# Last tower layer of a Fourier network: two of the square convolutions moved to its very beginning, one into each mix step, and unread TensorE products on both sides of the join

## The reference

```python
for i in range(L):                                   # L = 4
    x1 = _fourier_layer(v, W1, W2)                   # rfft2, 12 x 12 modes mixed, irfft2
    x2 = jnp.einsum('bcxy,cd->bdxy', v, w_w[i]) + w_b[i][None, :, None, None]
    v = x1 + x2
    mean = jnp.mean(v, axis=(0, 2, 3), keepdims=True)
    var = jnp.var(v, axis=(0, 2, 3), keepdims=True)
    v = (v - mean) * jax.lax.rsqrt(var + BN_EPS)
    v = v * bn_g[i][None, :, None, None] + bn_b[i][None, :, None, None]
    if i < L - 1:
        v = jax.nn.relu(v)
out = jnp.einsum('bcxy,cu->bxyu', v, q_w) + q_b
```

## Time and profile before

| | us |
|---|---|
| median of 3 runs | 854.49 (853.65 to 860.16) |
| profiled execution, its time | 850.2 |
| profiled execution, its span | 848.4 |
| TensorE busy | 665.2 (78%) |
| VectorE busy | 561.2 (66%) |
| ScalarE busy | 361.2 (43%) |
| L696 (convolutions, 512 instructions), busy | 45.6 |

### The profile page before, as it was taken

How to read it: one execution, slowest core, us unless ns; L and a number is a source line. 1 busy time by engine, 2 the same in 40 slices (tenths; PEclk the granted TensorE clock), 3 DMA queues, 4 the chain that set the end, 5 groups by cost and what they waited for, 6 DMA issues and landing times. The chain is left out here.

```text
span 848.4 us, 22240 instructions
## 1 busy us (share of the span) xinstructions
PE 665.2 (78%) x10155; PEld 443.9 (52%) x10155; DVE 561.2 (66%) x858; ACT 361.2 (43%) x485; POOL 49.6 (6%) x88
## 2 busy tenths in 40 slices
PE   3889927776899276678992999777967979797997
PEld 2867613336676132376761334234365858685854
DVE  7859878973688799736887797224047675547453
ACT  0025569100255591002555775331034646364753
POOL 3100000002000000110000000200010202010200
PEclk9989968996899699958996899755987989677999
DMA  8400000023000000320000000400040000000001
GB/s 303 92 2 3 3 0 2 1 87 141 2 2 2 1 1 2 129 98 2 3 2 1 2 2 2 150 20 3 14 179 1 3 1 1 1 1 1 1 1 27
DMA packets 12270, 27.28 MB, mean 32 GB/s; under 512 B 3472, under 2 KB 4368, under 8 KB 12176
## 3 DMA queue, kind: packets, MB, share of 16 engines
q1 hardware_dynamic: 11888, 25.12, 8.8%
q10 hardware_dynamic: 288, 0.73, 0.2%
HBM read 24.80 MB, written 1.05 MB: 30 GB/s over the span
## 5 line engine op out<-in xcount | busy, mean ns | idle before, releaser
L438 ACT ACTIVATE V<-ps,wts 128x1024 f32<-128x1024 f32 x96 | 101.8, 1111 | 252.8 <-PE ps L784 252.8
L612 DVE BATCH_NORM_STATS2 stats<-V 128x6 f32<-128x512 f32 x192 | 117.9, 676 | 15.8 <-ACT V L438 15.6
L488 DVE STREAM_TRANSPOSE A<-V 128x2048 f32<-128x2048 f32 x48 | 107.2, 2273 | 6.7 <-ACT V L389 6.7
L684 PE MATMUL ps<-A,tab 128*128 128x384 f32 x192 | 75.4, 532 | 30.6 <-DVE A L495 30.6
L389 ACT ACTIVATE V<-V,small 128x2048 f32<-128x2048 f32 x48 | 96.6, 2082 | 5.0 <-DVE small L640 5.0
L672 PE MATMUL ps<-A,tab 32*32 32x512 f32 x1536 | 66.6, 654 | 33.8 <-DVE A L488 33.8
L606 DVE STREAM_TRANSPOSE A<-ps 128x2048 f32<-128x2048 f32 x24 | 55.5, 2315 | 36.2 <-PE ps L769 36.1
L684 PEld LDWEIGHTS ps<-A,tab 128*128 128x128 f32 x192 | 36.0, 201 | 80.7 <-DVE A L495 57.4
L784 PEld LDWEIGHTS ps<-tab,A 64*128 64x128 f32 x1024 | 62.5, 195 | 28.0 <-issue 28.0
L495 DVE STREAM_TRANSPOSE A<-ps 128x1024 f32<-128x1024 f32 x48 | 56.7, 1220 | 20.1 <-PE ps L672 20.1
L784 PE MATMUL ps<-tab,A 64*128 64x128 f32 x1024 | 68.8, 286 | 0.0
(11 more groups left out here) (229 smaller groups left out, 919.6 us busy)
## 6 DMA issues: line engine op xcount, KB each, us to landing
A<-in_modes SPq DMA_DIRECT2D x32, 384.0 KB, 6.5
r_ky<-in_modes SPq DMA_DIRECT2D x16, 384.0 KB, 6.4
wl<-in_layers SPq DMA_DIRECT2D x3, 452.0 KB, 5.7
wm<-in_mixture SPq DMA_DIRECT2D x1, 874.5 KB, 8.0
tab<-in_table SPq DMA_DIRECT2D x1, 656.5 KB, 4.9
A<-in_turned SPq DMA_DIRECT2D x1, 512.0 KB, 3.9
V<-in_pixels SPq DMA_DIRECT2D x4, 128.0 KB
tower_out<-A SPq DMA_DIRECT2D x2, 256.0 KB, 2.0
```

The costliest lines, as they stand in the source:

```text
L438: nc.scalar.activation(Vm[:, 2 * h:2 * h + 2, r, 512 * q:512 * (q + 1)], bank(half_of_u(q, r) + 2 * h, 2).rearrange("p (m n) -> p m n", m= ...
L488: nc.vector.transpose(T[n % 3].rearrange("p (k n) -> p k n", k=16), Vk[:, :, P * n:P * (n + 1)]).then_inc(s_T, 1)
L612: last = nc.vector.bn_stats(stats[:, 16 * q + 4 * r + m, :], Vm[:, m, r, 512 * q:512 * (q + 1)])
L684: last = nc.tensor.matmul(bank(4 + (2 * (u % 2) if l < L - 1 else 0) + pair)[:, 0:MODES * CH], fwd_x[layout][ri], y[:, :, MODES * ri:MODES ...
```

## The change

The eight pieces that were left for the mix are split: two (`early`) go to the very beginning of the layer, six (`late`) into the mix steps, one in each, between L739 and L752. The pieces in the units are three as before, numbered from 2 on. On ScalarE the two first squares stand behind `relu(2)`, and each step has one square and one energy. Two groups of three products of a constant table with a constant matrix are added, whose result (in bank 7) nobody reads: one behind the last square's semaphore and ahead of the join's first product, one behind that product.

```diff
@@ -260,9 +260,13 @@
+        early = 2 * PAIRS - 3 * FU - KYP
+
         def squares_in(u):
 
-            return range(3 * u, 3 * u + 3) if u < FU else range(3 * FU, 2 * PAIRS)
+            return range(early + 3 * u, early + 3 * u + 3)
+
+        late = 2 * PAIRS - KYP
@@ -407,17 +411,19 @@
                 if l == L - 1:
-                    for n in range(6):
+                    for n in range(3):
+                        relu(n)
+                    for m in range(early):
+                        square(m)
+                    for n in range(3, 6):
                         relu(n)
...
-                    rest = squares_in(FU)
                     for k in range(KYP):
-                        for m in rest[2 * k:2 * k + 2]:
-                            square(m)
+                        square(late + k)
                         energy(k)
@@ -700,6 +706,9 @@
                 if l:
                     pe.wait_ge(s_norm, l)
+                    if l == L - 1:
+                        for m in range(early):
+                            convolve(m)
                     forward_y(0)
@@ -721,9 +730,6 @@
-                    if l == L - 1:
-                        for m in squares_in(FU)[2 * k:2 * k + 2]:
-                            convolve(m)
                     pe.wait_ge(s_rky, l * MODES + 2 * k + 2)
@@ -740,6 +746,7 @@
                     if l == L - 1:
 
+                        convolve(late + k)
                         if k:
                             pe.wait_ge(s_Z, KYP * l + k + 1)
@@ -831,8 +838,16 @@
+            def warm(n):
+
+                for _ in range(n):
+                    nc.tensor.matmul(bank(7), first, tab[:, 0:512], start=True, stop=True)
+
+            pe.wait_ge(s_square, 2 * PAIRS)
+            warm(3)
             pe.wait_ge(s_bn, 3 * (L - 1) + 2)
             nc.tensor.matmul(bank(6)[:, 0:2], average, small[:, 2:4], start=True, stop=True).then_inc(s_join, 1)
+            warm(3)
             pe.wait_ge(s_p, 1)
```

## The result

| | before | after |
|---|---|---|
| median of the runs measured together | 854.07 us (4 runs) | 827.08 us (822.05, 822.31, 831.85, 838.96) |
| ratio, 95% interval | | 0.965 (0.955 to 0.975) |
| profiled execution: span | 848.4 us | 820.5 us |

The change saved 27 us where 9 were forecast. The time is 1.4 us from that of the first rival (828.5, the clock never falls).

The account below looks back on a forecast made before the run. Bound: TensorE and VectorE handing over without slack, convolutions waiting for ScalarE's squares, the mix at 1.2 GHz. Sum 2.0 - 5.9 - 5.0 - 0.5 + 0.2 = -9.2: median 845.3 us, own range 841.5 to 849, 8 in 10 827 to 850.

Parts of the forecast that it names:

- first rival: Mix: the clock stays at 2.4 GHz instead of falling, steps of about 3.2 us, time 828.5; chance 0.20.
- Head, +2.0: Layer's beginning: the second early convolution delays the first y-transform by 2.3 us, partly given back; +2.0, ends +0.8 and +2.3.
- more work earlier can bring the clock up earlier: Head: reason given for the lower end, +0.8, of the +2.0 us term.
- Between loop and mix, -5.9: Passage from loop to mix: two waiting convolutions leave, so the mix starts at 539.33 instead of 545.22; -5.9 us.
- Mix, -5.0 and -0.5: Mix: six steps of 5.95 us at low clock, 35.7 against 40.7; another -0.5 for a first step partly at high clock.
- this kind of work doesn't raise a clock that is low: Mix: premise, read from TensorE busy 2.00 of 2.00 us at 0.50, that steps stay at 1.2 GHz; the sum used it.
- The rule that I weighed against the row: Mix: skill's rule that continuously busy TensorE reaches full clock, giving the 2.4 GHz time 828.5; set aside for the profile's clock row.
- Tail, +0.2: Join: first three unread products add 2.1 us, the spectra products at high clock save 1.9; +0.2 us.
- The wait that comes back: Mix steps: each convolution waits for its square behind the previous step's energy; 863 us with 3 us waits; chance 0.03.

Follow-up runs that it names:

- e2: Kernel before with only the two groups of unread products added, convolutions in their old places; ratio 0.998.
- e7: Changed kernel without the two early convolutions: all eight inside the mix steps, two each in steps 0 and 1; ratio 0.989.
- e5: Changed kernel with TensorE held ahead of the first mix product by eight ScalarE activations, so the mix starts at the low clock; ratio 0.984.
- e14: Changed kernel with TensorE held ahead of the mix by eight ScalarE activations, profiled a second time; 837.7 us.
- e15: Changed kernel with TensorE held ahead of the mix by eight ScalarE activations, profiled a third time; 825.4 us.
- e6: Changed kernel with the six late convolutions and squares two by two ahead of steps 0 to 2, early ones and unread products kept; ratio 0.998.
- e8: Changed kernel with each late convolution ahead of its step's mix products instead of behind them; ratio 0.987.
- e1: Changed kernel without both groups of unread products; ratio 0.969.
- e9: Changed kernel measured once more, nothing altered; ratio 0.976.
- e3: Changed kernel with the six late convolutions and squares left out; executions 821.74, 824.07, 806.91 and 830.03 us.
- e12: Changed kernel without the six late convolutions and squares, the gap ahead of the loop's last convolution filled with an unread product; ratio 0.973.
- e4: Changed kernel with one unread product put into the 1.4 us gap ahead of the loop's last convolution; ratio 0.964.
- e11: Changed kernel with two unread products in the gap ahead of the loop's last convolution and two ahead of each early convolution; ratio 0.974.
- e13: Changed kernel with the gap filled and four unread whole-array products in place of each convolution in the mix, squares left out; ratio 0.989.

## Why the prediction was wrong

Point by point, with distances from the layer's first ReLU, since that came 2.3 us earlier for reasons outside the change:

- **Head, +2.0: measured -0.2.** The start of the second convolution was right (7.24 us after the first ReLU; forecast 7.2). Wrong was the clock behind it. Convolution and y-transform took 4.6 us together (462.85 to 467.44), where I had added 1.89 and 4.08. At 1.2 GHz they would have taken about 6.3 (an estimate: 2.9 us at 0.50 and twice the 1.7 at 1.00), so the sum was right for the low clock; but the clock was back at about 465.8, and before it was 0.50 until 473. VectorE's turn moved by 0.9 (11.87 against 10.96) instead of 2.3. The first x-transforms ran at 2.4 GHz too, and the first unit gave back 1.08 (8.96 us instead of 10.04), of which I had deducted 0.3. I had allowed for this ("more work earlier can bring the clock up earlier") with an end at +0.8 only. But that the early convolutions bring the clock back isn't shown: it comes back 10.2 us after the first ReLU here, 10.1 to 13.4 in the twelve other profiles that have them and no filled wait at the head, and 15.3 in the kernel before and 15.1 in e2, but 10.0 in e7, which has none. Against e7, with the clock back at the same time, the way to the mix is 1.5 us longer (81.24 against 79.72): that is what the early convolutions cost, near the +2.0 of the forecast, and the measured -0.2 owes the rest to when the clock came back. The y-transform began 7.42 us after the ReLU, 0.57 later than before, in between the convolution's products. The Trainium skill, "TensorE: Matmul & The Clock Gate", section "Why this matters for your kernels", says that products on small tiles at different places of the array run at the same time; the trace agrees in that the two lines, both on 32*32 tiles, overlap at their start, but not in that the pair became cheaper than its sum.
- **Between loop and mix, -5.9: measured -5.9** (-6.1 with the head in it).
- **Mix, -5.0 and -0.5: measured -17.7** (23.0 against 40.7). The size at 1.2 GHz was right: e5 has 5.88 us a step. The failed step is the sentence that "this kind of work doesn't raise a clock that is low", and the weight of 0.20 that I gave the first rival for it. I had drawn it from a mix with a wait in each of its first steps, and from two microseconds near its end. The runs showed instead a mix granted 1.00 for 22.11 of its 26.26 us up to the join, the clock back from 0.50 within the first step, and in e14 and e15 the same mix raising a clock that was low at its start. By the same row I read one wait of 1.37 us at the passage as if it were as bad as two; profiles with two or three such waits in succession (before, e2, e6, e8) all fell there, those with one (after, e1, e9, e3) held the clock or had it back within a step (e3 lost it again in the second).
- **The rule that I weighed against the row.** The same section of the Trainium skill says that a continuously busy TensorE gets to full clock. In the changed kernel the trace agrees (busy for 20.36 of 22.11 us, granted 1.00), and by the rule the time would have been right within 2 us. It isn't the whole: in e8, e12 and e5 TensorE was busy for 22.0, 17.6 and 40.4 us without a gap to speak of and was granted 0.50 (0.52 in e12). The row showed one of two things that happen, the rule tells of the other.
- **First rival.** Its time, 828.5, is 1.4 us from the measured one, in part by luck: its head was 2.2 us too long and its steps 2.8 too short. Its steps were put at 3.4 us on average and measured 3.8: 4.8 with the short fall, 4.2 with a wait, then 3.2 to 3.75; "one us for VectorE's extra work behind the first step" is the 0.76 us ahead of L759 at 545.02. Its tail of -1.6 was, between mix end and join, +0.4 (3.2 against 2.8) and then -2.1.
- **Tail, +0.2: measured -1.7.** With the clock at 2.4 GHz three unread products take 2.84 us; forecast 3.1 at this level and 5.9 at the other, for which e5 has 5.19. L859 to L870 is 1.96 us, forecast 1.9.
- **The wait that comes back** in the steps didn't; e7 shows its price where two convolutions stand in one step: 1.37 us, and the clock with it.

Of 27.9 us of span, 25.6 lie in the three stretches that the change touches, 3.0% of 848.4. The ratio of 0.970 that this makes lies between the two measured ratios, 0.965 and 0.976. What stays open is what decides in a single execution whether a mix without gaps is raised at once (e14, e15), after 24 us (e8) or not at all (e5): e5, e14 and e15 are one kernel, e8 differs in the order of a step. No version here is faster than the changed kernel by more than can be measured.

## What to carry to other kernels

Where a stage stands at the low clock, ask first whether it has short waits, at its entry above all, and price the case that they go, though no run here shows how long or how many waits it takes: in the mix the shorter order alone was worth some 5 us (six steps of 5.88 in e5, 35.3 against 40.7) and the clock another 12. A trace of a stage with gaps doesn't show what the same instructions do without them. Compare executions stage by stage before comparing medians, for a stage far from the change may have two lengths of its own.

## What the runs showed of the hardware beyond that

- Work without a gap runs at either level, and for long: 100 TensorE instructions in 10 us at 1.00 or in 19 us at 0.50 in the transformer, in two executions of the same program; 40.40 of 40.40 us busy at 0.50 in e5.
- Lengths of the part behind the join come in two groups, 257.4 to 259.5 and 266.3 to 267.0 us, and nothing between.
- Products of two neighbouring lines on 32*32 tiles start interleaved (462.85, 463.03, 463.67, 463.85), but the pair costs about its sum: some 6.3 us at 1.2 GHz in the changed kernel and 6.0 in e9 (estimates from the time at each level) against 1.89 + 4.08.
- The clock that is low at the layer's start comes back at different times in one kernel: 10.2 and 11.9 us after the first ReLU in the two profiles of the changed kernel.
- Gaps of up to 1.15 us within the mix products (e4, e11) left the clock at 1.00.
- At 2.4 GHz an unread product of 512 columns (fp32) on the whole array takes 0.93 us when several follow one another (3.70 us for four in e13).
